# A state-space mixer's first stage and scan, rebuilt by channel, with the outputs returned by DMA

## The reference

```python
def _L0_attn_ref(hidden_states, W_in, conv_w, conv_b, log_dt, ..., D, W_out):
    H, N = 256, 8                                  # channels, complex states of each
    xz = jnp.einsum('bld,ed->bel', hidden_states, W_in)
    x, z = jnp.split(xz, 2, axis=1)                # 256 channels each
    x = conv_general_dilated(pad(x, 3), conv_w)    # 4 taps, by channel
    x = silu(x + conv_b)
    k = 2.0 * einsum('hn,hnl->hl', Ct, exp(dtA * t)).real    # kernel of 512 steps
    y = irfft(rfft(x, 1024) * rfft(k, 1024))[..., :512]      # causal long convolution
    y = (y + x * D) * silu(z)
    return jnp.einsum('bhl,dh->bld', y, W_out)

def _L0_ffn_ref(x, gate_w, gate_b, expert_bias, w1, b1, w2, b2):
    top_idx = argmax(x @ gate_w.T + gate_b + expert_bias)    # one of 8 experts a token
    return (relu(x @ w1[top_idx] + b1[top_idx])) @ w2[top_idx] + b2[top_idx]

x = layernorm(x + _L0_attn_ref(x, ...))
x = layernorm(x + _L0_ffn_ref(x, ...))
```

## Time and profile before

| what | value |
|---|---|
| three runs | 266.8, 268.2, 268.19 us |
| their median | 268.19 us |
| profiled execution, span of its trace | 263.8 us |
| its own time beside the span | not given; the median is taken for it |
| busy, share of the span: PE | 239.2 us, 91% |
| ACT | 187.1 us, 71% |
| DVE | 177.0 us, 67% |
| POOL | 139.8 us, 53% |
| first stage, until the first product of the scan | 0 to 80 us |
| scan | 80 to 131 us |
| output projection, dispatch, experts | 131 to 264 us |

### The profile page before, as it was taken

How to read it: one execution, slowest core, us unless ns; L and a number is a source line. 1 busy time by engine, 2 the same in 40 slices (tenths; PEclk the granted TensorE clock), 3 DMA queues, 4 the chain that set the end, 5 groups by cost and what they waited for, 6 DMA issues and landing times.

```text
span 263.8 us, 8892 instructions
## 1 busy us (share of the span) xinstructions
PE 239.2 (91%) x2763; PEld 215.1 (82%) x2764; DVE 177.0 (67%) x552; ACT 187.1 (71%) x528; POOL 139.8 (53%) x208
## 2 busy tenths in 40 slices
PE   8999979999999899999979999359989999999970
PEld 4888768888887678888869999349979999899960
DVE  1889995997218657777724878842877676566672
ACT  2999999856998778888655665207667777667740
POOL 6000000400009989999624687878746656657545
PEclk9999999999999999999999999759999999999995
DMA  7697884600399999999293221647865676677600
GB/s 232 180 313 288 346 334 150 244 0 0 105 310 332 310 279 296 308 320 302 66 361 120 93 93 41 212 92 191 220 179 172 200 210 164 203 195 208 189 34 6
DMA packets 54267, 52.06 MB, mean 197 GB/s; under 512 B 4415, under 2 KB 42817, under 8 KB 54114
## 3 DMA queue, kind: packets, MB, share of 16 engines
q1 hardware_dynamic: 51506, 46.65, 59.2%
q0 software_dynamic: 2304, 4.34, 4.6%
q10 hardware_dynamic: 432, 0.79, 0.8%
HBM read 38.14 MB, written 14.07 MB: 198 GB/s over the span
## 4 chain that ended last, share of the span: by engine, by line
PE 59%; DVE 10%; ACT 10%; POOL 9%; issue 6%; DMA 5%; SPq 1%; DVEq 0%; ACTq 0%; POOLq 0%
PE banks L1292 13%; PE banks L1477 9%; PE banks L1487 8%; PE banks L1370 7%; POOL dispatched_rows L568 5%; ACT BR L672 5%; PE banks L1380 5%; PE banks L1384 4%; PE banks L1275 3%; PE banks L1357 3%; PE banks L1435 2%; DMA X<-dispatched_rows 2%; POOL RE L558 1%; DMA out<-X 1%; POOL out L576 1%
## 5 line engine op out<-in xcount | busy, mean ns | idle before, releaser
L515 POOL TENSOR_TENSOR Wx<-BR,RE 128x384 f32 (+1 forms) x32 | 47.9, 1548 | 27.9 <-PE banks L1292 26.6
L1292 PE MATMUL banks<-Wx,XT 128*128 128x256 f32 x256 | 59.9, 380 | 1.7 <-ACT Z L643 1.7
L809 ACT ACTIVATE Z<-banks,BR 128x128 f32<-128x128 f32 x156 | 44.6, 368 | 18.4 <-PE banks L1477 18.3
L1292 PEld LDWEIGHTS banks<-Wx,XT 128*128 128x128 f32 x256 | 48.4, 190 | 9.0 <-issue 2.2
L576 POOL DMA_INDIRECT out<-X x39 | 38.4, 986 | 27.8 <-DVE X L1233 15.3
L1477 PE MATMUL banks<-Z 128*128 128x128 f32 x312 | 42.7, 281 | 0.4 <-ACT Z L798 0.2
L1487 PE MATMUL banks<-BR,Z 128*128 x312 | 41.1, 276 | 1.2 <-DVE X L1216 1.2
L1477 PEld LDWEIGHTS banks<-Z 128*128 128x128 f32 x312 | 39.0, 196 | 1.0 <-issue 0.5
L1487 PEld LDWEIGHTS banks<-BR,Z 128*128 128x128 f32 x312 | 37.8, 192 | 1.5 <-issue 1.5
L568 POOL DMA_INDIRECT dispatched_rows<-TR,CR x32 | 31.0, 970 | 9.3 <-POOL RE L558 9.3
L1057 DVE TENSOR_TENSOR X<-banks,Z 128x256 f32 (+1 forms) x32 | 20.4, 636 | 9.1 <-PE banks L1384 9.1
(11 more groups left out here) (220 smaller groups left out, 469.6 us busy)
## 6 DMA issues: line engine op xcount, KB each, us to landing
TR<-kernel_rows SPq DMA_DIRECT2D x32, 512.0 KB, 6.5
Z<-w SPq DMA_DIRECT2D x39, 256.0 KB, 3.1
dispatched_rows<-TR SPq DMA_DIRECT2D x3, 2310.0 KB, 8.8
X<-dispatched_rows SPq DMA_DIRECT2D x39, 66.0 KB, 2.1
XT<-hidden_t SPq DMA_DIRECT2D x10, 256.0 KB, 3.1
RE<-decay_and_turns SPq DMA_DIRECT2D x2, 1024.0 KB, 7.4
BR<-w SPq DMA_DIRECT2D x1, 2048.0 KB, 8.2
dispatched_rows<-TR SPq DMA_DIRECT2D x1, 1848.0 KB, 7.8
```

What stands on the lines that cost most here:

```text
L515: nc.gpsimd.tensor_tensor(BC[:, k, 0:LAGS, :].rearrange("p m (s r n) -> p (m s) r n", s=STRIPS, r=2), Btab[:, :, :, :, :, one].rearrange(" ...
L809: last = nc.scalar.activation(HT[:, j, c * P:c * P + P], bank[UP_BANKS[j]][:, c * P:c * P + P], ACT.Relu, bias=B1[:, bass.ds(experts[j] * ...
L1292: last = mm(bank[X_BANKS[k]][:, j * CHAN:(j + 1) * CHAN], XT[:, slot, at:at + CHUNK], Wx[:, tap, :], start=(tap == 0), stop=(tap == TAPS - 1))
```

## The change

**x by channel, projected once.** Now the weights are stationary and 512 tokens of one batch move. A unit u is one half of the channels (j = u // 8) of one batch: one product of 512 columns (`project_x`). ACT writes the last tap and the bias into `xc` (`last_tap`), DVE adds the other three taps, shifted along the free axis, out of PSUM (`add_taps`), PE transposes the four chunks (`turn_x`), ACT writes SiLU of it into `X` (`keep_x`). z is 16 products of 512 columns, and ACT writes SiLU(z) with channels on the partitions (`keep_z`). All eight batches stay in SBUF.

**States.** Powers are built from 28 angles a group in place of 129: 16 fine steps, 8 coarse ones, three lags and a half angle; `expand` multiplies coarse by fine ones into `Etab`, DVE for the groups 0 to 15, POOL for 16 to 31. POOL also does the chain of small operations for the amplitudes (`Z0`, `Z1`), `Sel` and the turning matrices `Rot`. PE transposes `Etab` into `ET` (`turn_powers`). In the scan `sum_local` sums each chunk's own states for four groups, ACT copies them (`keep_local`), `turn_states` turns and adds those of earlier chunks by products with 32 x 32 tiles, and DVE writes them, masked, into `V` (`states`).

**Outputs.** `convolve` and `add_states` add into the same bank, chunks on the partitions. ACT copies the result (`keep_y`) into a ring of four and issues two transfers from SBUF to SBUF (`send_y`), each from 128 partitions to four: a row of 128 steps for each channel, batch and chunk goes to its channel's partition, in `Y0` (groups 0 to 15) or the first half of `X` (16 to 31). So the outputs lie with channels on the partitions; the transposes and copies after the scan are gone, and the gate is a product over 512 columns a batch (`gate`, DVE) or, for `Y0`, one over all (POOL).

**Order.** The scan is written out in full, in 8 turns of 4 groups. The x units 8 to 15, the second half of the kernel rows and of the turned powers are put between the groups of the turns 0 to 2. The kernel rows are stored in two halves. The four fills of the slot table go from SP's queue to POOL's; POOL waits for them before it uses their source's memory again.

The core of the diff, the old lines left out where the text above tells them:

```diff
@@ sync
+            def store_rows(j):
+                sp.wait_ge(s_kx, 2 * j + 2)
+                sp.dma_start(kext[j * P:(j + 1) * P, :], Kx[:, j, :]).then_inc(s_kd[j], 16)
+                sp.wait_ge(s_kd[j], 16)
+            def load_toeplitz(g):
+                wait_past(sp, s_tm, g - (T_SLOTS - 1))
+                sp.dma_start(Tring[:, g % T_SLOTS, :, :], toeplitz[:, g * GH:(g + 1) * GH, :]).then_inc(s_t[g % T_SLOTS], 16)
+            store_rows(0)
+            for g in range(T_SLOTS):
+                load_toeplitz(g)
+            store_rows(1)
+            for g in range(T_SLOTS, GROUPS):
+                load_toeplitz(g)
+            sp.wait_ge(s_y, GROUPS)
             sp.dma_start(B1, b1).then_inc(s_b1, 16)
             sp.dma_start(W2.rearrange("p e q -> p (e q)"), w2).then_inc(s_ew, 16)
@@ gpsimd
+            for turns in FILLS:
+                pool.dma_start(rows_of[:, filled:filled + turns, :],
+                               empties.unsqueeze(1).to_broadcast([P, turns, FILL_ROWS * ROW])).then_inc(s_fill, 16)
+                filled += turns
...
+            done(tt(v(DEN), v(EA_SQ), v(AI_SQ), ALU.add))
+            pool.wait_ge(s_tanh, 1)
+            ts(v(OMT), v(TH), -0.5, 0.5, ALU.mult, ALU.add)
+            ts(v(DEN), v(DEN), 0.5, None, ALU.mult).then_inc(s_den, 1)
...
+            turning(slice(0, HALF))
+            part = slice(HALF, GROUPS)
+            pool.wait_ge(s_far, 1)
+            expand(nc.gpsimd, Etab[:, part, :], part, first_coarse, cosine)
+            done(expand(nc.gpsimd, products[:, part, :], part, second_coarse, sine))
+            tt(Etab[:, part, :], Etab[:, part, :], products[:, part, :], ALU.add).then_inc(s_e1, 1)
+            pool.wait_ge(s_fill, 16 * len(FILLS))
+            nc.gpsimd.memset(EN[:, 1024:2048], 0.0).then_inc(s_v0, 1)
+            turning(slice(HALF, GROUPS))
...
+            for k in range(Y_RING):
+                pool.wait_ge(s_yd[k], HALF // Y_RING * 32)
+            pool.wait_ge(s_z, BATCH)
+            tt(Y0[:, :], Y0[:, :], Z[:, 0:TOKENS], ALU.mult).then_inc(s_g0, 1)
@@ scalar
+            def keep_y(g):
+                act.wait_ge(s_y, g + 1)
+                wait_past(act, s_yd[g % Y_RING], g // Y_RING * 32)
+                nc.scalar.activation(YT[:, g % Y_RING, :].rearrange("p (j u) -> p j u", j=2), backwards(6 + g % 2, CHUNK - 1, 2),
+                                     ACT.Copy).then_inc(s_yt, 1)
+            def send_y(g):
+                half, at = g // HALF, g % HALF
+                act.wait_ge(s_yt, g + 1)
+                for j in range(2):
+                    if half:
+                        home = bass.AP(X[:, :, :].tensor, (j * 64 + at) * CHAN * TILES, [[16 * CHAN * TILES, 4], [P, TILES], [1, P]])
+                    else:
+                        home = bass.AP(Y0[:, :].tensor, (j * 64 + at) * TOKENS, [[16 * TOKENS, 4], [P, TILES], [1, P]])
+                    act.dma_start(home, YT[:, g % Y_RING, j * P:(j + 1) * P]).then_inc(s_yd[g % Y_RING], 16)
@@ vector
+            def add_taps(u):
+                j = u // BATCH
+                dve.wait_ge(s_x3, u + 1)
+                for back in range(1, TAPS):
...
+                    stt(xc[:, u % 2, back:], bank[u % 2][:, 0:SEQ - back], channel[:, j, TAPS - 1 - back:TAPS - back],
+                        xc[:, u % 2, back:], ALU.mult, ALU.add).then_inc(s_xk, 1)
...
+            dve.wait_ge(s_den, 1)
+            nc.vector.reciprocal(v(RDEN), v(DEN))
...
+            expand(nc.vector, Etab[:, part, :], part, first_coarse, cosine)
+            done(expand(nc.vector, products[:, part, :], part, second_coarse, sine))
+            tt(Etab[:, part, :], Etab[:, part, :], products[:, part, :], ALU.add).then_inc(s_e0, 1)
@@ tensor
-                    for tap in range(TAPS):
-                        at = chunk * CHUNK + tap
-                        last = mm(bank[X_BANKS[k]][:, j * CHAN:(j + 1) * CHAN], XT[:, slot, at:at + CHUNK], Wx[:, tap, :],
-                                  start=(tap == 0), stop=(tap == TAPS - 1))
+            def project_x(u):
+                wait_past(pe, s_xk, (u - 1) * LAGS)
+                pe.wait_ge(s_xt[b], 16)
+                mm(bank[u % 2], Win[:, j * P:(j + 1) * P], XT[:, b, :], start=True, stop=True).then_inc(s_x, 1)
+            def turn_x(u):
+                pe.wait_ge(s_xk, (u + 1) * LAGS)
+                wait_past(pe, s_xe, u)
+                for chunk in range(CHUNKS):
+                    at = slice(chunk * P, (chunk + 1) * P)
+                    last = nc.tensor.transpose(bank[2][:, at], xc[:, u % 2, at], ident[:, :])
+                last.then_inc(s_xtr, 1)
...
+            def convolve(g):
+                pe.wait_ge(s_t[g % T_SLOTS], (g // T_SLOTS + 1) * 16)
+                wait_past(pe, s_yt, g - 1)
+                for h in range(GH):
+                    at, part = h // 4 * P, h % 4 * TILES
+                    last = mm(yt[part:part + TILES, at:at + P], X[:, g * GH + h, :], Tring[:, g % T_SLOTS, h, :],
+                              start=(h < 4), stop=False)
+                last.then_inc(s_tm, 1)
+            def add_states(g):
+                pe.wait_ge(s_v, g + 1)
+                for j in range(2):
+                    last = mm(yt[:, j * P:(j + 1) * P], V[:, g % V_RING, j * 4:j * 4 + 4, :].rearrange("p h t -> p (h t)"),
+                              Etab[:, g, :], start=False, stop=(j == 1))
+                last.then_inc(s_y, 1)
```

More of the change, by code:

```diff
@@ new lines, in _ @@
+            nc.scalar.activation(cosine[:, :, :], cosine[:, :, :], ACT.Sin, scale=-TWO_PI, bias=quarter[:, :]).then_inc(s_sin, 1)
+            nc.scalar.activation(ssq[:, 0, 0:1], epscol[:, :], ACT.Silu).then_inc(s_silu, 1)
+            last_tap(1)
+            for i in range(10):
+                keep_z(i)
+            keep_x(0)
+            last_tap(2)
+            for i in range(10, 13):
+                keep_z(i)
+            keep_rows(0)
+            keep_powers(0)
+            keep_powers(1)
@@ new lines, in _ @@
+            keep_z(13)
+            keep_x(1)
+            last_tap(3)
+            keep_powers(2)
+            keep_powers(3)
+            keep_x(2)
+            last_tap(4)
+            keep_z(14)
+            keep_x(3)
+            last_tap(5)
+            keep_z(15)
+            for u in range(4, BATCH):
+                keep_x(u)
+                last_tap(u + 2)
+            act.wait_ge(s_rot, 1)
+            keep_local(0)
+            act.wait_ge(s_e1, 1)
+            keep_x(8)
+            last_tap(10)
@@ L764, in squares @@
+            send_y(GROUPS - 1)
             def squares(s):
@@ new lines, in _ @@
+            dve.wait_ge(s_ch, 16)
+            add_taps(0)
+            dve.wait_ge(s_fell, 1)
+            for at, table in ((1, sine), (2, cosine)):
+                dve.wait_ge(s_sin, at)
+                tt(table[:, :, 0:DECAYED], table[:, :, 0:DECAYED], fall[:, :, 0:DECAYED], ALU.mult).then_inc(s_dwn, 1)
+            dve.wait_ge(s_dwn, 2)
+            far = slice(FINE, FINE + COARSE)
+            done(ts(coarse_part[:, :, :], sine[:, :, far], odd, None, ALU.mult))
+            done(stt(first_coarse[:, :, :], cosine[:, :, far], even, coarse_part[:, :, :], ALU.mult, ALU.add))
@@ new lines, in _ @@
+            for u in range(1, 9):
+                add_taps(u)
+            dve.wait_ge(s_v0, 2)
+            for g in range(4):
+                states(g)
+            add_taps(9)
+            add_taps(10)
+            dve.wait_ge(s_v0, 3)
+            for g in range(4, 8):
+                states(g)
+            add_taps(11)
+            add_taps(12)
+            for g in range(8, 12):
+                states(g)
+            for u in range(13, UNITS):
+                add_taps(u)
+            dve.wait_ge(s_late, 48)
@@ L1062, in _ @@
             ts(centre[:, 0:DM], ident[:, :], 1.0 / DM, None, ALU.subtract).then_inc(s_ctr, 1)
             tt(gbias[:, 2, :], gbias[:, 0, :], gbias[:, 1, :], ALU.add).then_inc(s_ctr, 1)
-            states(0, 0)
-            states(0, 1)
-            output(0, 0)
-            with dve.Fori(1, GROUPS // 2) as r:
-                states(r, 0)
-                output(r - 1, 1)
-                states(r, 1)
-                output(r, 0)
+            for g in range(12, 20):
+                states(g)
@@ L1077, in _, with gate @@
               .then_inc(s_wox, 1)
+            for g in range(24, GROUPS):
+                states(g)
+            def gate(n):
+                if n < QUADS:
+                    at = slice(n * SEQ, (n + 1) * SEQ)
+                    tt(Y1[:, at], Y1[:, at], Z[:, TOKENS + n * SEQ:TOKENS + (n + 1) * SEQ], ALU.mult).then_inc(s_g1, 1)
             def scale(s):
@@ L1185, in rows_of_blocks @@
                 dve.wait_ge(s_first, 2 if at else 1)
-            dve.wait_ge(s_yc, GROUPS + LEAD)
+            for k in range(Y_RING):
+                dve.wait_ge(s_yd[k], GROUPS // Y_RING * 32)
+            dve.wait_ge(s_z, UNITS)
+            gate(0)
+            gate(1)
             dve.wait_ge(s_cconst, 2)
```

(17 more changed lines are left out.)

1103 lines of the change are left out of this document (469 added, 634 removed).

## The result

The changed kernel takes 305.7 us (median of four runs, 301.7 to 309.8) against 267.5 for the kernel before: a ratio of 1.132, interval 1.122 to 1.143 (it leaves out the two runs that lie over 1.5% above the fastest; the mean of the other two is 303.2). Slower, as forecast, but by 36 us and not by 7, and outside the range. The profiled execution has a span of 300.0 and a time of 301.72, so the margin beside the span is 1.7 us and not the 4.4 that was taken from the median. Against the forecast span of 270.8, 29.2 us are missing: the last output lands 23.4 later than forecast (162.9, not 139.5), the part behind is 5.5 longer (136.1, not 130.6), and the gate with its waits 0.3.

The account below looks back on a forecast made before the run. PE and the transfer engines bound the old scan, a tenth apart. Last output at 139.5 on four full lanes, plus gate 0.7 and untouched rest 130.6, gave a 270.8 us span; with a 4.4 margin 275, range 258 to 300.

Parts of the forecast that it names:

- the margin beside the span: Kernel time beyond the profiled span: 4.4 us, from the earlier median 268.19 over span 263.8, added to reach 275.
- The start of the scan: End of the rebuilt first stage: DVE's chain brings the scan's first products to 48 us, bounds 44 to 58, instead of 80.
- Rival C: First stage: POOL's slow fills or 4 ns an element move the scan's start from 48 to 58, time 285; chance 0.15.
- The cause: Scan outputs' way back: a send to four rows uses only four of sixteen lanes, setting 2.9 us a group; chance 0.55.
- 24 x 1.5 + 30 x 1.4 = 78, to 133: Scan from 55 us: 24 remaining Toeplitz tiles at 1.5 us and about 30 groups' sends at 1.4 on the same four lanes.
- PE's scan: PE's work in the scan: 32 groups at 1.30 us plus 13 us moved from the first stage, 55 us against 50.
- I take 5 of it: Scan's end: expert weights cost each lane 7.8 us beside the last queued sends, of which 5 us were counted.
- 1.5 of landing: Scan's end: a 66 KB transfer lands 2.1 us after issue, of which 1.5 us were counted, giving 139.5.
- Isn't touched: Dispatch and experts after the scan: assumed unchanged at 130.6 us.
- 4 ns an element: POOL's two-input operations in the first stage: upper price, making four large ones take 31 us, until 58; half was taken.
- Rival A: Scan: sends are hidden at 0.39 us a group or less, PE and ACT set the pace, time 243; chance 0.18.
- Rival B: Scan: two of a send's four rows share a way in, send pair 2.6 us not 1.4, time 311; chance 0.12.

Follow-up runs that it names:

- the shape with 128 rows: The changed kernel with the same output sends, but each landing one piece in each of 128 rows instead of 32 pieces in four (wrong output): 281.6 us.
- price to DRAM: The changed kernel with its four-row output sends written in the same shape to DRAM instead of SBUF, nothing reading them: 295.0 us, 3.04 us a group.
- late weights: The changed kernel with the expert weights (2.6 MB) asked for only after all sends have landed: 294.6 us; with PE products of no use and moved transposes, 298.4 us.
- mixed pair: Changed kernel with groups 8 to 23 returned through DRAM, the others straight to neighbouring rows, plus other edits: 287.4 us with PE products of no use, 291.0 without.
- POOL's sends: The changed kernel with its sends issued by POOL instead of ACT and the first half gated by DVE: 300.2 us; with further edits 290.6.

## Why the prediction was wrong, point by point

**The start of the scan: right.** The first Toeplitz product runs at 46.4 (forecast 48). DVE waited 2.3 us for POOL's denominator, until 11.6 and not 16; the four fills cost POOL 1.0 us each. Rival C falls. That the sum came so near is in part luck: the 4.4 us gained there were partly lost in a wait of DVE's that the forecast didn't have, 2.82 us at 29.9, behind kernel rows for which PE had waited for POOL until 27.6.

**The cause: right.** A send of four rows is carried by four lanes. The closing packets, the busy share of 0.26, the shape with 128 rows and the nearly unchanged price to DRAM agree. So does the rule of the Trainium skill ("DMA: Bandwidth & Descriptors", section "Why a DMA increments its semaphore by 16 and not by 1").

**The step that failed: "24 x 1.5 + 30 x 1.4 = 78, to 133".** The path was right, tiles and sends one behind the other on four lanes; the prices were too low. They were taken from the scan's first 10 us (334 GB/s) and its best single microsecond (367). The windows behind them, with the lanes nearly as full, have less:

```profile
90.00:100.00 10.00, 8.95 (x264) 7.23 (x256) 6.20 (x12) 7.25 (x21) 8.69 (x7) 1.00 1.01 282
100.00:110.00 10.00, 10.00 (x308) 8.31 (x307) 7.12 (x14) 8.75 (x26) 10.00 (x7) 1.00 1.07 290
110.00:120.00 10.00, 10.00 (x308) 8.23 (x306) 7.26 (x14) 8.33 (x25) 10.00 (x8) 1.00 1.10 319
```

- At their mean of 297 GB/s a tile costs each lane 1.76 us and not 1.5. Sends alone ran at 70 and 78 GB/s (windows from 139 to 146, and from 150 to 156 with late weights), that is 17.5 and 19.5 on each of four lanes where the sum had 23: 1.7 to 1.9 us a group and not 1.4. Tile and sends make 3.4 to 3.6, and 3.38 were measured, where the forecast had 2.9.
- With 1.76 and 1.7 the same sum is 24 x 1.76 + 30 x 1.7 = 93 and ends at 148: 15 us more. With late weights, where nothing collides with them, the last sends land at 156.1; the forecast has 134.5 for that (133 and 1.5 of landing). So the prices are 15 of 21.6 us. The other 7 weren't traced one by one; that no send had moved by 55, so that 32 groups were left and not 30, is 3 of them.
- PE's scan was mis-sized as well, but it isn't what cost the time. The prediction had 55 us, 1.30 a group and 13 for the moved work. Without any transfer it measures 71 (from 47 to 118.5): 0.57 for a Toeplitz product in place of 0.46, 0.64 for the states' in place of 0.43, 0.37 for sums and turning, 1.6 in all, and the moved half takes the first ten groups until 85. The chain is PE's until then, but the four lanes were full beside it from 55 on (106%).

**"I take 5 of it" and 1.5 of landing: nearly right.** From last copy to last landing it took 13.4 us. Late weights show 6 to 7 of it to be the collision, for the 5 of the forecast; the rest is sends that were still queued, and belongs to the sum above.

**"Isn't touched": not so.** The part behind took 136.1 us from its first product in place of 130.1. PE, which before came from transposes at full clock, now comes from a wait, and from 163 to 175 its clock is 0.64. Full clock gave back 4.4 us in the mixed pair and 2.2 with late weights (135.7 to 133.5), so the clock is a good part of the 6 and needn't be all of it.

**Rival A** failed on its own price too: with the sends not only hidden but gone the time is 259.3, so the rebuilt first stage and scan are worth 8 to 10 us, not 25. **Rival B** holds at most in sign: 0.34 us a group between DRAM and rows 16 apart, far from 1.2.

No version that returns the outputs beats the kernel before. What the first stage earns is spent again. The scan starts 33 us earlier; PE alone then needs some 73 us until the projection in place of 54 (from 80.0 to 133.7), which leaves the 13.9 of the kernel without transfers beside it (119.8 for 133.7). Tiles and sends put 44 on top (163.95), the part behind, with its clock, 6. That is 36 us, the whole distance of the spans, 300.0 and 263.8.

## What to carry to other kernels

Before moving data by DMA to a few rows, count the lanes that will carry it, and read a mean transfer share of 0.7 as possibly four full lanes. Price a lane by its mean rate over the whole stage that it bounds, not by that stage's best window: this was most of the error here. And where a wait is put ahead of a matrix stage that stays as it is, price that stage at the lower clock.

## What the runs showed of the hardware

**PE's waits for nothing shown end behind transfers of instructions.** In the kernel without sends the chain has them inside the turning (98.06) and after two of the four products of a group's states (108.34):

```profile
98.06 1.91 issue
...
108.34 1.93 issue
110.27 0.38 PE banks L1261 x2
```

With eight tiles and no other transfer the second is there as well, but lasts 0.29:

```profile
105.36 0.29 issue
105.65 0.38 PE banks L1259 x2
```

With POOL's sends the same two places last 5.00 and 3.85 (109.48 and 125.52). The trace also records when the queue of instructions (q8: 19 transfers of 16 KB, 11 in the kernel before) moves one. Such a transfer ended at 98.5 and 108.8 in the first kernel, at 104.3 in the second, at 112.4 and 127.4 with POOL's sends: each of these five waits ends 1.4 to 2.1 us after it. All the runs together have 59 waits of over 0.25 us between two products of PE in the chain from 46 to 140 us, and every one ends 1.0 to 2.2 us behind the end of a 16 KB transfer of this queue. That fits a written-out program whose own code comes late. That these transfers bring PE's code is argued from the times, since the record doesn't name an engine. Busy transfer engines make some of these waits longer, but aren't needed for one: at 71 us it lasts 1.43 with a share of 0.02, 1.17 without sends, 2.80 with POOL's.

**POOL's small operations stood still beside DVE's large ones.** Three operations of POOL over 32 elements took 2.25 to 2.36 us each, and the next 0.25; DVE's three over 2,048 run at just these times:

```profile
18.71 2.25 POOL L531 TENSOR_TENSOR EN<-EN 128x32 f32<-128x32 f32 x1
20.93 2.29 POOL L532 TENSOR_TENSOR EN<-EN 128x32 f32<-128x32 f32 x1
23.19 2.36 POOL L533 TENSOR_TENSOR EN<-EN 128x32 f32<-128x32 f32 x1
25.51 0.25 POOL L534 TENSOR_TENSOR EN<-EN 128x32 f32<-128x32 f32 x1
```

```profile
18.56 2.29 DVE L340 TENSOR_TENSOR CR<-Y 128x2048 f32<-128x2048 f32 x1
20.77 2.34 DVE L340 TENSOR_TENSOR X<-Y 128x2048 f32<-128x2048 f32 x1
23.15 2.29 DVE L941 TENSOR_TENSOR CR<-CR,X 128x2048 f32<-128x2048 f32 x1
```

The Trainium skill ("SBUF — State Buffer", section "SBUF: two separate sides") has the two engines share a pair of ports that one holds for a whole instruction. The trace agrees. These waits, some 6 us together, lie on the chain ahead of the kernel rows, for which PE waited until 27.6.

POOL's own three operations over 2,048 elements took 3.7, 3.7 and 4.5 us; by the 4 ns an element of the prediction's bound they would have taken 8.2 each. The Trainium skill ("GPSIMD Engine Reference", section "Performance versus the Vector engine") gives 4,497 ns for one. The trace has one within 1% of that and two 18% below.
